# One order of five groups of small matmuls against another, in a linear-attention block on one Trainium2 core

## The reference

```
q, k, v = heads(x @ Wq.T + bq), heads(x @ Wk.T + bk), heads(x @ Wv.T + bv)    # 16 heads of 32
q, k = exp(q), exp(k)
kv  = cumsum(k[..., :, None] * v[..., None, :], axis=sequence)
k1  = cumsum(k, axis=sequence)
num = einsum('zsD,zsDd->zsd', q, kv)
den = sum(q * k1, axis=-1)
x = layernorm(x + (num / den) @ Wo.T + bo)
x = layernorm(x + tanh(((x @ weight) @ aux_weight1) @ aux_weight2 + bias))
```

## Time and profile before

| | |
|---|---|
| time, median of 3 runs | 2330.29 us (2329.91 to 2331.95) |
| the profiled execution: its own time | 2327.62 us |
| the profiled execution: span of the instructions | 2325.9 us |
| TensorE matmuls busy | 2242.6 us (96%) |
| TensorE weight loads busy (beside the matmuls) | 1830.6 us (79%) |
| VectorE / GpSimd / ScalarE busy | 1603.7 / 1290.4 / 1008.9 us |
| granted TensorE clock, mean | 0.992 |
| one slot in the loop | 17.22 us |

### The profile page before, as it was taken

One profiled execution on the slowest core, in us unless ns is written; L12 is line 12 of the kernel. 1 busy time (PEld: TensorE's weight loads), 2 busy tenths in 40 slices (PEclk: granted clock), 3 DMA queues, 4 the chain that ended last, 5 costly groups with the idle time before them and its releaser, 6 DMA issues.

```text
span 2325.9 us, 77275 instructions
## 1 busy us (share of the span) xinstructions
PE 2242.6 (96%) x27752; PEld 1830.6 (79%) x27752; DVE 1603.7 (69%) x2444; ACT 1008.9 (43%) x1683; POOL 1290.4 (55%) x1797
## 2 busy tenths in 40 slices
PE   3999999999999999999999999999999999999985
PEld 2777888888888888888888888888888888788864
DVE  3477677776776776777767767777677677677674
ACT  2344444444444444444444444444444444444442
POOL 1255555556555555555565555555655655555554
PEclk9999999999999999999999999999999999999997
DMA  6133333333333333333333333333333333333221
GB/s 160 44 98 109 111 107 110 107 111 109 104 110 110 106 110 106 111 110 106 107 114 102 111 109 108 109 104 114 110 103 108 112 106 109 107 102 114 69 69 55
DMA packets 294478, 243.15 MB, mean 105 GB/s; under 512 B 33329, under 2 KB 225841, under 8 KB 294193
## 3 DMA queue, kind: packets, MB, share of 16 engines
q1 hardware_dynamic: 294192, 238.69, 33.1%
HBM read 139.99 MB, written 98.57 MB: 103 GB/s over the span
## 4 chain that ended last, share of the span: by engine, by line
PE 94%; DVE 2%; issue 1%; ACT 1%; DMA 1%; POOL 1%; SPq 0%; POOLq 0%; DVEq 0%; ACTq 0%
PE SC L314 26%; PE SC L315 25%; PE SC L316 25%; PE SC L400 6%; PE ND L374 5%; PE ND L365 3%; PE ND L361 2%; PE ND L411 2%; DVE o L719 0%; PE ND L314 0%; PE ND L316 0%; PE ND L315 0%; DMA KT<-wkT 0%; DMA QT<-wqT 0%; ACT A L601 0%
## 5 line engine op out<-in xcount | busy, mean ns | idle before, releaser
L805 POOL TENSOR_SCALAR_AFFINE_SELECT A<-A 128x512 f32<-128x512 f32 x512 | 330.0, 677 | 307.9 <-ACT A L601 307.8
L719 DVE RECIPROCAL o<-ND 128x512 f32<-128x512 f32 x128 | 427.7, 3341 | 0.0
L776 DVE TENSOR_TENSOR xres<-SC,xres 128x512 f32<-128x512 f32 x128 | 88.5, 692 | 425.0 <-PE SC L316 424.8
L799 POOL TENSOR_TENSOR oL<-o,oH 128x512 fp32r<-128x512 f32 x128 | 165.8, 1295 | 325.9 <-ACT oH L580 325.9
L591 ACT ACTIVATE WK<-xres,shift,rstd 128x512 f32<-128x512 f32 x128 | 104.1, 813 | 524.1 <-POOL shift L845 524.1
L601 ACT ACTIVATE A<-SC 128x512 f32<-128x512 f32 x512 | 264.7, 605 | 43.9 <-PE SC L400 43.9
L314 PE MATMUL SC<-xTH,WqH 128*128 128x512 f32 x512 | 210.4, 411 | 30.5 <-POOL xTL L834 27.0
L834 POOL TENSOR_TENSOR xTL<-xin,xTH 128x512 fp32r<-128x512 f32 x128 | 165.4, 1293 | 90.9 <-ACT xTH L629 90.9
L314 PE MATMUL SC<-WfH,x1H 128*128 128x512 f32 x512 | 200.7, 392 | 14.4 <-issue 7.9
L732 DVE TENSOR_TENSOR_SCAN WK<-ones,k,KT 128x128 f32<-128x128 f32 x512 | 207.7, 468 | 8.3 <-PE ND L361 8.3
L314 PE MATMUL SC<-WoH,oH 128*128 128x512 f32 x512 | 201.0, 393 | 9.7 <-issue 7.8
(11 more groups left out here) (100 smaller groups left out, 4996.9 us busy)
## 6 DMA issues: line engine op xcount, KB each, us to landing
xin<-x SPq DMA_DIRECT2D x512, 64.0 KB, 1.9
xres<-x SPq DMA_DIRECT2D x128, 256.0 KB, 2.7
x_rows<-WK SPq DMA_DIRECT2D x128, 256.0 KB, 3.3
WK<-x_rows SPq DMA_DIRECT2D x512, 64.0 KB, 2.0
out<-WK SPq DMA_DIRECT2D x128, 256.0 KB, 2.1
k_rows<-WK SPq DMA_DIRECT2D x120, 256.0 KB, 2.0
WK<-k_rows SPq DMA_DIRECT2D x480, 64.0 KB, 2.1
QT<-wqT SPq DMA_DIRECT2D x4, 256.0 KB, 4.4
```

The lines of the kernel that those rows point to most:

```text
L719: nc.vector.reciprocal(o[:, :, :], den_ps).then_inc(recip_ready, 1)
L799: nc.gpsimd.tensor_tensor(oL[:, :, :], o[:, :, :], oH[:, :, :].bitcast(F32), ALU.subtract).then_inc(ol_ready, 1)
L805: last = nc.gpsimd.affine_select(out=A[:, k % 2, j, :, :], in_=A[:, k % 2, j, :, :], compare_op=ALU.is_ge, fill=0.0, base=0, pattern=[[0, ...
```

## The change

The groups of the small block come in another order: AV of tile k - 1, scores of tile k, product with the state of tile k - 1, denominators of tile k - 1, state update of tile k - 2. In PSUM the product with the state is now added to AV, where AV was added to it. The waits move with the groups: `o_ready` and `state_ready` now stand ahead of AV, `qk1_ready` ahead of the product. One semaphore, `nd_done`, given by the last denominator matmul, takes the place of `den_done` and `num_done`. AV of a tile is now issued ahead of the next tile's scores, so A needs one buffer in place of two; `qk1` now has two, and the scan on VectorE waits for the denominators of a tile earlier. No instruction is added or taken away.

The core of the diff (places where only a name changes are left out):

```
             def attend(c, n):
                 wait(pe, v_ready, c.count(n + 1))
                 wait(pe, masked, c.count(n + 1))
+                wait(pe, o_ready, c.count(n))
+                wait(pe, state_ready, c.state_count(n - 1))
                 for j in range(HG):
                     for g in range(NK):
...
-                                                A[:, n % 2, j, g, :], start=not c.reads_state(n),
-                                                stop=True, skip_group_check=True)
-                last.then_inc(num_done, 1)
+                                         A[:, j, g, :], start=True, stop=not c.reads_state(n),
+                                         skip_group_check=True)
             def denominators(c, n):
-                wait_before(pe, (qk1_ready, c.count(n + 1)), (o_ready, c.count(n)),
-                            (state_ready, c.state_count(n - 1)))
-                for g, j, quarter, h in heads:
-                    last = nc.tensor.matmul(den_ps[quarter, j, :], ones[h, :], qk1[h, g, :], start=True, stop=True)
-                last.then_inc(den_done, 1)
+                wait_before(pe, (qk1_ready, c.count(n + 1)))
                 if c.reads_state(n):
                     for g, j, quarter, h in heads:
                         nc.tensor.matmul(num_ps[quarter, j, :], state[h, n % B, g, :], QT[h, ts, g, tcols],
-                                         start=True, stop=False, skip_group_check=True)
+                                         start=False, stop=True, skip_group_check=True)
+                for g, j, quarter, h in heads:
+                    last = nc.tensor.matmul(den_ps[quarter, j, :], ones[h, :], qk1[h, n % 2, g, :],
+                                            start=True, stop=True)
+                last.then_inc(nd_done, 1)
...
                 if att and prev:
-                    denominators(c, k - 1)
+                    attend(c, k - 1)
...
                     last.then_inc(scores_done, 1)
                 if att and prev:
-                    attend(c, k - 1)
+                    denominators(c, k - 1)
...
                     wait(act, scores_done, c.count(k + 1))
-                    wait(act, num_done, c.count(k - 1))
...
-                    wait(dve, den_done, c.count(k))
+                    wait(dve, nd_done, c.count(k - 1))
```

More of the change, by code:

```diff
@@ L74, in linear_attention_ffn_kernel @@
         V = sb("V", [P, 2, D])
-        A = sb("A", [P, 2, HG, NK, P])
-        WK = sb("WK", [P, 8, D])
+        A = sb("A", [P, HG, NK, P])
+        WK = sb("WK", [P, 9, D])
         y = WK[:, 0:2, :]
@@ L81, in linear_attention_ffn_kernel @@
         x1s = WK[:, 6, :]
-        qk1 = WK[:, 7, :].rearrange("p (g q) -> p g q", g=NK)
+        qk1 = WK[:, 7:9, :].rearrange("p s (g q) -> p s g q", g=NK)
         o = sb("o", [P, NK, P])
@@ L109, in linear_attention_ffn_kernel @@
         qproj_ps, kproj_ps, v_ps, oproj_ps, ffn_ps = SC[:, 0, :], SC[:, 1, :], SC[:, 2, :], SC[:, 3, :], SC[:, 0, :]
-        den_done, scores_done, oproj_done, qproj_done, num_done, kproj_done, state_done, ffn_done, v_done = [
-            sem(n) for n in ("den_done", "scores_done", "oproj_done", "qproj_done", "num_done", "kproj_done",
+        scores_done, oproj_done, qproj_done, nd_done, kproj_done, state_done, ffn_done, v_done = [
+            sem(n) for n in ("scores_done", "oproj_done", "qproj_done", "nd_done", "kproj_done",
                              "state_done", "ffn_done", "v_done")]
@@ L352, in _, with attend @@
                      for g in range(NK) for j in range(HG)]
+            def attend(c, n):
+                wait(pe, v_ready, c.count(n + 1))
+                wait(pe, masked, c.count(n + 1))
+                wait(pe, o_ready, c.count(n))
+                wait(pe, state_ready, c.state_count(n - 1))
+                for j in range(HG):
+                    for g in range(NK):
+                        f0 = g * P + j * HD
+                        nc.tensor.matmul(num_ps[g * HD:(g + 1) * HD, j, :], V[:, n % 2, f0:f0 + HD],
+                                         A[:, j, g, :], start=True, stop=not c.reads_state(n),
+                                         skip_group_check=True)
             def denominators(c, n):
                 ts, tcols = (n // QUAD) % 2, slice(n % QUAD * P, (n % QUAD + 1) * P)
-                wait_before(pe, (qk1_ready, c.count(n + 1)), (o_ready, c.count(n)),
-                            (state_ready, c.state_count(n - 1)))
-                for g, j, quarter, h in heads:
-                    last = nc.tensor.matmul(den_ps[quarter, j, :], ones[h, :], qk1[h, g, :], start=True, stop=True)
-                last.then_inc(den_done, 1)
+                wait_before(pe, (qk1_ready, c.count(n + 1)))
                 if c.reads_state(n):
@@ L604, in slot @@
                     wait(act, qproj_done, c.count(k + 5))
-                    wait(act, num_done, c.quad_count(k - 4))
+                    wait(act, nd_done, c.quad_count(k - 4))
                     nc.scalar.activation(QT[:, ns, b, :], qproj_ps, ACT.Exp,
@@ L714, in normalise @@
                 def normalise(n):
-                    wait(dve, num_done, c.count(n + 1))
+                    wait(dve, nd_done, c.count(n + 1))
                     wait(dve, oh_ready, c.count(n))
```

21 lines of the change are left out of this document (7 added, 14 removed).

## The result

| | before | after |
|---|---|---|
| time, median of 7 runs each, in turn | 2330.29 us (2329.14 to 2333.47) | 2338.98 us (2337.84 to 2339.21) |
| profiled execution: own time, span | 2327.62, 2325.9 us | 2337.84, 2336.1 us |
| one slot in the loop, median | 17.228 us | 17.347 us |

The changed kernel takes 1.0033 times the time of before (95% interval 1.0021 to 1.0044): slower by 8.7 us. The prediction said 2338.0 (2330 to 2344) and slower with a chance of 0.66.

What follows compares the result with a forecast made beforehand. TensorE, busy 96% of the span, was taken to bound the kernel. Full slots' +11.3 and early slots' -3.3 us sum to +8.0 on 2327.62, so 2335.6; with 2.7 for the median, 2338 us, range 2330 to 2344.

Steps and rivals of the forecast that it cites:

- item 1: Front of the small block: AV hides in the scores' wait for VectorE; scores' load at 1.33 us against 1.32, cost +0.01.
- item 2: Scores in the small block: 0.91 us from weight load to last start, unchanged.
- items 3 and 4: Behind the scores: product and denominators take 0.80 us, state update 0.27; with shape changes 1.59 against 1.50.
- rival A: Scores to product: a change of columns alone costs 0.09 us, not 0.20; 2325 us, chance 0.08.
- rival B: Behind the scores: product and denominators both run at the first group's pace, pair 0.55 us; 2310 us, chance 0.05.
- C: Small block: scores pinned at 1.32 us, state update 0.24; slot +0.06, total 2333.5 us, chance 0.15.
- D: State update: stays at issue pace with its load exposed, 0.31 us; slot +0.14, total 2343 us, chance 0.12.
- as those of the first end: Second 32 x 32 group: its matmuls can only be issued as the first group's end, so 0.48 us against 0.23.
- item 5: Slot count: 113 full slots at +0.10 us cost 11.3; slots 2 to 8 at -0.47 each give -3.3.
- item 6: Moved waits and changed buffers: AV's waits long satisfied, VectorE held by its own queue, no buffer cost; all at nothing.

Runs made afterwards that it cites:

- run 3: Also before_no_product_spread: the kernel before without the product of queries and state, padding spread over three places; 2339.98 us, 1.0040.
- run 8: Also six_changes: the changed kernel reordered to denominators, AV, scores, product, state update; 2344.87 us, 1.0069 times the kernel before.
- run 9: Also pair_apart: the changed kernel reordered to AV, scores, denominators, state update, product; 2330.38 us, 1.0006 times the kernel before.
- run 5: Also old_addresses: the changed kernel with every tensor, A and `qk1` included, at its address from before; 2344.50 us, 1.0063 times the kernel before.
- su_behind_av: Also run 6: the changed kernel with the state update moved right behind AV, ahead of the scores; 2346.50 us, 1.0070 times the kernel before.
- run 7: Also su_waits_ahead: the changed kernel, state update right behind AV, the scores' waits except `z_ready` moved ahead of AV; 2330.46 us, 1.0000 times before.
- after_no_product_spread: The changed kernel without the product of queries and state, padding spread over three places; 2303.01 us, 0.9886 times the kernel before.

## Why the prediction was right, step by step

**AV in front, hidden** (item 1). Right. 0.318, 0.808 and 0.203 put the scores' first start at 1.329 against 1.325. That what VectorE's reading pins is the place, and not the work in front of it, is shown by run 3: 1.33 with and without the product.

**Scores unchanged** (item 2). Right, 0.903 in both.

**Behind the scores** (items 3 and 4). Forecast 1.59 as 0.20 + 0.80 + 0.20 + 0.27 + 0.12; measured 0.200 + (0.249 + 0.069 + 0.482) + 0.197 + 0.263 + 0.124 = 1.584. The change of columns alone (scores to product), which the trace of before did not have, costs 0.20, so rival A falls. The second group is slow also behind the long scores, so rival B falls. The state update takes 0.263, inside the bounds of 0.24 and 0.31 and between C's and D's ends. That the place makes the second group slow, and not the group, is shown: each of the two is slow when second (product before 0.482, denominators after 0.482) and fast when it stands behind another shape (product 0.249 and 0.248 in runs 8 and 9). The reason I gave for it is not shown. In either kernel single starts lie mostly 7 ns apart in the first group; in the second the next start comes 0.11 us behind the first one, and the others in steps of 16 to 17 ns, one or two to a step. The first group's matmuls, all of one length, end 7 ns apart too, so "as those of the first end" does not give this pace. And the second group takes the same 32 x 32 places of the array as the first, which could hold it as well; no run parts the two.

The Trainium skill (TensorE: Matmul & The Clock Gate, Part 3, The mechanism) gives a 64-deep window of loads and matmuls; a group is 32 of each, and by that figure, as I read it, a second group would be issued only as the first one makes room. Runs 8 and 9 agree in that a parted group is fast (0.249 and 0.248 against 0.482), but none of them counts the window or tells it from the places in the array.

**The loop** (item 5). The slot is 0.119 longer by the median and 0.099 by the mean, against 0.10, and slots 9 to 121 cost 11.11 us against 11.3. The match is better than the reasoning, and in part luck. The block's 0.084 makes 9.5 us; the slow start of the large matmuls, which no item of mine had, adds 113 x 0.035 = 4.0; and 2.4 is given back by fewer slots with a hiccup. For the whole execution the forecast summed +8.0, the profiled pair shows +10.2 and the medians +8.7.

**The early slots** (item 5), the step that was mis-sized. Forecast -3.3 for slots 2 to 8. Measured for slots 1 to 8: +0.91 - 1.62 + 1.25 - 1.74 = -1.20. Where nothing else disturbs (slots 4 to 8) each gave 0.35. I had put ScalarE's copy at 0.94 behind the scores' last start and so "just behind" TensorE's 1.02; the copy decides at 1.19. I read the copy's end (0.33 + 0.61) rightly, since its signal comes 0.95 behind that start in run 8, and left out what lies between it and TensorE's first matmul: the two wait instructions, 0.11 apart, and the load. Run 8 shows the same 1.19 in another order. The rest of the miss is slot 1, where AV meets V's copy, and the clock in slot 2.

**Waits and buffers** (item 6). Right in the loop: VectorE's inversion follows its own queue in both, and run 5 shows that A's and `qk1`'s places change neither block nor slot. Wrong for slot 1: the argument that AV's own waits are long satisfied was made from a slot in the loop and does not hold for the first tile.

**Rivals C and D.** The block grew by 0.084, between C's 0.06 and the forecast's 0.10. That the time came out at the forecast all the same is due to the slow start of the large matmuls and the smaller gain of the early slots, which no sum of mine held.

What stays open is that slow start. From the second large matmul behind the block on, ten steps lie, against 227 ns each, 9 ns too far in sum before, 43 after and in old_addresses, 19 in su_behind_av, 56 in su_waits_ahead, 38 and 37 in six_changes and pair_apart, 20 and 3 in before_no_product_spread and after_no_product_spread. It follows neither the shape ahead of it, nor the number of changes, nor the addresses of A and `qk1`. I have no theory that fits all of them.

## What to carry to other kernels

Price small groups by their neighbours, not by their instructions: here a change of array shape costs 0.13 to 0.21 us from the last start, and a second group of 32 loads and 32 matmuls right behind another of the same kind costs 0.23 more than the first, so keeping equal shapes together was dearer than parting them, though parting took one change more (run 9 against after). Before moving work, ask what wait it lies in: the one that comes out of the wait costs time again (0.43 us a slot here), and the one that goes in must fit, also in the first slots, whose copies and clock are not those of the loop. And look at the order's cheap parts, the waits and the padding: satisfied waits cost 0.09 us a slot (run 6 against run 7), two wait instructions stand between ScalarE's signal and the next load, and padding grown by an unrelated edit cost 279 us (2618.55 against 2339.98).

## What the runs showed of the hardware that I had not expected

- Instructions that do nothing are not free on TensorE: those of the padding stand 71 ns apart, and 64 instructions a slot fewer (32 matmuls, 32 loads) made the kernel 12% slower (2618.55 us); one padding had grown by 64, and with the padding spread it took 2339.98.
- Satisfied semaphore waits in TensorE's stream widened a gap from 0.126 to 0.261 us; each wait instruction stands 0.11 to 0.15 us from the next. Ahead of AV, behind a large matmul, they cost nothing: 0.318 from there to AV, as in the changed kernel.
- The gap at a change of shape is measured from the last start and depends on the matmul in front: 0.197 to 0.206 behind matmuls that stream 128 columns, 0.126 behind those of 32 columns. It is the same for a change of rows, of columns or of both. The Trainium skill (TensorEngine Tiling (Array Packing), Key Properties) says that changing the tiling mode drains TensorE; the traces agree in that all seven kinds of change seen have this gap, though none shows what TensorE does in it.
- After 1.97 us of idle in slot 2 of the changed kernel the granted clock was 0.50 (1.2 GHz) for 2.8 us. Of seven kernels that idled 1.96 to 2.05 us there five lost the clock, and began to at different times: the first large matmul 0.43 us from the next was the third in the changed kernel, and the sixth in pair_apart. Of the four that idled 0.82 to 1.58 none did.
